# A rounding moved from VectorE to ScalarE in the edge loop of a graph transformer

## What is computed

```python
rel_t = last_update[src] - t
rel_t_enc = jnp.cos(rel_t[:, None] * time_w[None, :] + time_b)      # 32 values for each edge
edge_attr = jnp.concatenate([rel_t_enc, msg], axis=-1)              # 32 + 64
k = k_all[src].reshape(-1, HEADS, CH);  v = v_all[src].reshape(-1, HEADS, CH)
e = (edge_attr @ We).reshape(-1, HEADS, CH)
alpha = jnp.sum(q_all[dst].reshape(-1, HEADS, CH) * (k + e), axis=-1) / math.sqrt(CH)
ex = jnp.exp(alpha - segment_max(alpha, dst)[dst])
out = segment_sum((v + e) * (ex / segment_sum(ex, dst)[dst])[:, :, None], dst)
```

## Time and profile before

| | before |
|---|---|
| three runs, us | 9613.65, 9630.29, 9636.99 |
| median, us | 9630.29 |
| the profiled execution, us | 9621.89 |
| its span, first to last instruction, us | 9620.2 |
| mean granted TensorE clock | 0.825 |
| DVE busy, us (share) | 8650.1 (90%) |
| PE busy | 7559.8 (79%) |
| POOL busy | 6405.7 (67%) |
| ACT busy | 5089.7 (53%) |
| first layer's loop on DVE, from the first `ve_stage` to the last `sum_stage`, us | 378 to 4960 |

### The profile page before, as it was taken

The page is one execution under the profiler, slowest core; times in us unless marked ns, Lnnn a source line. Parts: engine busy times, 40 slices in busy tenths (PEclk is TensorE's granted clock), DMA queues, the critical chain, the costliest instruction groups (busy, mean ns, idle before and its releaser), DMA issues. The chain is left out here.

```text
span 9620.2 us, 272103 instructions
## 1 busy us (share of the span) xinstructions
PE 7559.8 (79%) x52868; PEld 7071.2 (74%) x52869; DVE 8650.1 (90%) x21303; ACT 5089.7 (53%) x20838; POOL 6405.7 (67%) x6871
## 2 busy tenths in 40 slices
PE   6477777887778777787757777888888888888865
PEld 2477777777777777777746777788888888888854
DVE  5899999999999999999987666799999999999968
ACT  2277777777777777777743333333333333333300
POOL 0477777777777777777735777777777777777720
PEclk8699999999999999999975555688888888887888
DMA  6477776777777777777732222455555555555554
GB/s 196 106 185 186 183 181 182 187 183 185 183 182 185 185 184 184 185 184 183 182 85 72 74 74 74 115 151 151 151 153 151 153 150 152 151 153 148 151 139 116
DMA packets 1631706, 1484.67 MB, mean 154 GB/s; under 512 B 792007, under 2 KB 1363043, under 8 KB 1631203
## 3 DMA queue, kind: packets, MB, share of 16 engines
q1 hardware_dynamic: 1374244, 848.34, 35.9%
q0 software_dynamic: 257088, 632.95, 23.6%
HBM read 1225.51 MB, written 254.87 MB: 154 GB/s over the span
## 5 line engine op out<-in xcount | busy, mean ns | idle before, releaser
L818 POOL DMA_INDIRECT kv<-kv_scratch,arena x3136 | 3110.7, 992 | 1272.7 <-issue 832.9
L870 POOL DMA_INDIRECT message_scratch<-ohT,idx x3232 | 3099.2, 959 | 1090.5 <-issue 952.6
L1262 ACT ACTIVATE ohT<-bank,kv 128x128 f32<-128x128 f32 x3232 | 921.1, 368 | 2613.5 <-PE bank L1064 1832.3
L1155 ACT ACTIVATE arena<-arena,weights 128x65 f32<-128x65 f32 x7040 | 1772.1, 337 | 10.7 <-PE bank L983 8.7
L1078 PE MATMUL bank<-oh,kve 128*128 128x128 f32 x8640 | 1377.6, 320 | 141.5 <-DVE arena L1842 108.1
L1064 PE MATMUL bank<-acc,oh 128*128 x6464 | 1287.0, 362 | 208.5 <-ACT ohT L1263 207.9
L1078 PEld LDWEIGHTS bank<-oh,kve 128*128 128x128 f32 x8640 | 1231.1, 224 | 164.9 <-issue 152.0
L1064 PEld LDWEIGHTS bank<-acc,oh 128*128 128x128 f32 x6464 | 1144.1, 266 | 253.5 <-issue 253.1
L983 PE MATMUL bank<-arena,oh 128*128 128x130 f32 x7040 | 1009.4, 288 | 317.1 <-DVE acc L1674 296.7
L983 PEld LDWEIGHTS bank<-arena,oh 128*128 128x128 f32 x7040 | 906.7, 200 | 377.4 <-ACT arena L1155 182.1
L964 PE MATMUL bank<-We,featT 96*128 96x128 f32 x7040 | 1067.3, 299 | 125.6 <-ACT featT L1162 122.1
(11 more groups left out here) (234 smaller groups left out, 12888.7 us busy)
## 6 DMA issues: line engine op xcount, KB each, us to landing
kve<-message_scratch SPq DMA_DIRECT2D x2160, 129.0 KB
kve<-nodes_scratch SPq DMA_DIRECT2D x880, 256.0 KB
feat<-in_edge_attr_dram SPq DMA_DIRECT2D x880, 96.0 KB
feat<-block_scratch SPq DMA_DIRECT2D x812, 98.0 KB
arena<-q_scratch SPq DMA_DIRECT2D x880, 64.0 KB
message_scratch<-ohT,idx POOLq DMA_INDIRECT x3232
kv<-kv_scratch,arena POOLq DMA_INDIRECT x3136
feat<-in_edge_attr_dram SPq DMA_DIRECT2D x880, 32.0 KB
```

The costliest lines, as they stand in the source:

```text
L818: pool.indirect_dma_start(kv[:, k, g, :], None, kv_d, bass.IndirectOffsetOnAxis(ap=group_rows[:, half, k * G + g, 0:1].bitcast(I32), axis= ...
L870: pool.indirect_dma_start(msg_d, bass.IndirectOffsetOnAxis(ap=idx[:, k, g:g + 1], axis=0), sum_ring[:, k % RING1, g, :], None).then_inc(s_ ...
L1155: op = act.activation(wv[:, st.k % 2, g, h, :], vR[:, st.k, g, h, :], ACT.Copy, scale=weights[:, st.k // ROUND, g, st.k % ROUND, h:h + 1])
L1262: act.activation(sum_ring[:, st.k % RING1, g, 0:C], banks[2 + st.k % 2][:, g * P:(g + 1) * P], ACT.Copy, scale=taken[:, st.k, g, 2:3])
```

## The change

The second angle operation, adding MAGIC, leaves DVE. ACT does it, as an Identity activation with a bias tile that holds MAGIC, in a new stage `whole_stage`, which stands behind `featc_stage` and ahead of `weigh_stage` in even iterations. It waits for the first angle operation and counts on a semaphore of its own, `s_whole`. Its result `turns` lies in SBUF (in `arena`), no longer in PSUM. DVE's last angle operation, now `angle(1)`, waits for `s_whole` and comes behind `product_stage`. ANG becomes 2.

```diff
+        magic = sb("magic", [P, 1])
...
+        turns = room(BATCH * G * TD).rearrange("p (b t) -> p b t", t=TD)
...
-        turns = banks[7][:, 2 * P:2 * P + BATCH * G * TD].rearrange("p (b t) -> p b t", t=TD)
...
-        ANG = 3
+        ANG = 2
...
+            def whole_stage(st):
+
+                act.wait_ge(s_ang, ANG * st.batch() + 1)
+                act.activation(turns[:, :, :], encodings(st), ACT.Identity, bias=magic[:, :]).then_inc(s_whole, 1)
...
-                    sines = [(sine_stage, 16)] if k % BATCH == 0 else []
+                    wholes, sines = ([(stage_of, 16)] if k % BATCH == 0 else [] for stage_of in (whole_stage, sine_stage))
...
-                    at(i, k, (arg_stage, 18), *smalls, (featc_stage, 15), (weigh_stage, 2), *sines, *gaps, *exps)
+                    at(i, k, (arg_stage, 18), *smalls, (featc_stage, 15), *wholes, (weigh_stage, 2), *sines, *gaps, *exps)
...
+            dve.memset(magic[:, :], MAGIC)
...
                     if n:
-                        dve.wait_ge(s_ang, done + n)
+                        dve.wait_ge(s_whole, st.batch() + 1)
...
-                    elif n == 1:
-                        wait(dve, s_ang, done)
-                        op = dve.tensor_scalar(t, a, MAGIC, None, ALU.add)
                     else:
                         op = dve.scalar_tensor_tensor(out=a, in0=t, scalar=MAGIC, in1=a, op0=ALU.subtract, op1=ALU.subtract)
...
-                    at(i, k, *turn[0], (ve_stage, 14), *turn[1], (block_stage, 0), (ke_stage, 14), *turn[2], (sum_stage, 0),
-                       (onehotT_stage, 15), *once(5, forward_stage), (product_stage, 13), *once(5, backward_stage), *once(4, run_stage, first_stage),
+                    at(i, k, *turn[0], (ve_stage, 14), (block_stage, 0), (ke_stage, 14), (sum_stage, 0),
+                       (onehotT_stage, 15), *once(5, forward_stage), (product_stage, 13), *turn[1], *once(5, backward_stage), *once(4, run_stage, first_stage),
```

More of the change, by code:

```diff
@@ L348, in build @@
         s_seg = sems("s_seg", MT // SEGMENT)
-        s_rows0 = sems("s_rows0", 2)
+        s_rows0, s_whole = sems("s_rows0", 2), sem("s_whole")
         s_segi, s_acc1 = (sem(n) for n in ("s_segi", "s_acc1"))
```

## The result

The changed kernel takes 9688.16 us (median of four, 9683.98 to 9705.89) against 9624.6 us for the kernel before, run beside it: a ratio of 1.0064, with a 95% interval of 1.0052 to 1.0075. It is **slower by 0.64%, some 60 us**, where 90 us less were forecast.

The account below looks back on a forecast made before the run. DVE was taken to bound the kernel, busy 95% of the first-layer loop. 166 us gained less 62 wait, 10 overlap and 4 waking gave 90 us less: 9540 us as median, range 9464 to 9645 for 8 in 10.

Parts of the forecast that it names:

- L1510's removal: DVE, first-layer loop: taking the rounding off saves 0.377 us in each of 440 batches, 166 us.
- the later sine: ACT's sine comes later, delaying PE's e product for DVE; costed at nothing, 2 us at most in iteration 6.
- Nothing else of DVE hides this: Claim that L1510's removal counts in full, 166 us, since DVE had no idle time around it.
- The move behind the multiplication: DVE's last angle operation, moved behind product_stage, costs what it cost, 0.33 us; nothing added, 4 us either way.
- The addition on ACT: The rounding takes 0.50 us on ACT, 0.43 us of its queue, 189 us in all, absorbed by ACT's idle time.
- the Trainium skill's rule against adds on ScalarE: Adds belong on VectorE; by the rule alone the change loses 35 us, chance 0.02, counted within rival 2.
- The wait for the rounding: DVE's last angle operation waits for ACT in iterations 4, 6, 12, 14: 62 us, plus 10 overlap and 4 waking.
- just used up: Iteration 6, rounds without a wait: the later sine needs 0.76 us against 0.74 spare; costed at nothing.
- Rival 2: PE's longer idle time brings 14 us more low clock each round, 165 us in all: 9705 us, chance 0.10.
- the three rivals: Wait takes it all, 9630 us (0.15); slower by PE's clock, 9705 (0.10); waits are hidden, 9464 (0.10).

Follow-up runs that it names:

- e13_early: e4_block with DVE's last angle operation moved back right behind ke_stage, ahead of block_stage's register load; 9885.61 us, ratio 1.0267 to the kernel before.
- e7_actonly: The kernel before plus one unused 128x256 Identity activation on ACT in each even iteration, at the rounding's place; 9651.98 us, ratio 1.0017.
- e1_head24: The changed kernel with the head of DVE's first-layer loop 24 slots further on, its closing branch 28 places behind a multiple of 256; 9579.02 us, ratio 0.9954.
- e4_block: e1_head24 with block_stage, a register load on DVE's sequencer, moved behind ke_stage; 9572.52 us, ratio 0.995 to the kernel before.
- e18_beforewarm: The kernel before with PE's e matmuls in iterations 1, 2, 9, 10 and aggregation matmuls in 4, 6, 12, 14 done twice; 9568.9 us, ratio 0.9948.
- e14_warm: e4_block with PE's e matmuls in iterations 1, 2, 9, 10 and aggregation matmuls in 4, 6, 12, 14 done twice; 9508.73 us, ratio 0.9875.
- e15_both: e4_block with the rounding first in ACT's even iterations, and the sine ahead of the weighings in iterations 6 and 14; 9511.78 us, ratio 0.9872.
- e17_all: e15_both with the doubled PE matmuls of e14_warm added; 9576.99 us, ratio 0.9957 to the kernel before.

## Why the prediction was wrong, step by step

The step that failed first is one that the prediction put at nothing without a word: that DVE's loop, 24 instructions shorter, otherwise runs as before. Its closing branch cost 96 us more. Behind it two terms of the sum were wrong: L1510's removal gave 41 us less than its 166, and the later sine, put at nothing, cost 28. The details:

- **L1510's removal, 166 us: right as a reading, 41 us too much as a gain.** 2.99 us a pass, 164 us, is what its start-to-start distances gave. "Nothing else of DVE hides this" was true, and the reverse had been left out: **L1510 hid something itself.** The prediction looked for idle time around L1510 and found none, because L1510 covered the register load of `block_stage` where the sequencer had no lead. That the 0.48 and 0.41 us in iterations 0, 2 and 10 were longer than the usual 0.33 was used for a larger gain, and it was the sign of the load beneath: 41 us. The rows of iteration 0 even have 0.06 us of idle time behind L1510 (2515.66 + 0.42 = 2516.08 against 2516.14).
- **The move behind the multiplication costs nothing: right**, L1516 takes 416 ns, and L1512 took 414. e13_early shows that it is worth some 300 us as against waiting behind `ke_stage`.
- **The addition on ACT, 0.50 us each: right; no effect of its own: nearly right.** The row after:

```profile
L1168 ACT ACTIVATE arena<-feat,magic 128x256 f32<-128x256 f32 x440 | 218.5, 497 | 7.4 <-DVE feat L1514 5.0 <-issue 1.1
```

  e7_actonly puts the added work alone at +0.17%, 16 us, at most 30. The prediction had drawn 35 us from the Trainium skill's rule against adds on ScalarE ("ScalarE: Activation LUTs", "Rules for kernel authors"); e7_actonly stays below this.
- **The wait for the rounding, 62 + 10 + 4 = 76 us: the size right** (0.97 x 55 = 53 us in the changed kernel, 62 in e1_head24), the places half right: iterations 6 and 14, as said, but nothing in 4 and 12, where 17 us had been put; only 0.15 us a pass of another kind was lost there. One in iteration 6 (DVE, then ACT):

```profile
2537.91 0.68 DVE L1545 TENSOR_TENSOR y_all<-kve,bank 128x512 f32<-128x512 f32 x1
2539.39 0.42 DVE L1516 SCALAR_TENSOR_TENSOR feat<-arena,feat 128x256 f32<-128x256 f32 x1 [0.80 <-ACT arena L1168]
```

```profile
2538.38 0.57 ACT L1163 ACTIVATE featT<-bank 96x512 f32<-96x512 f32 x1
2538.86 0.49 ACT L1168 ACTIVATE arena<-feat,magic 128x256 f32<-128x256 f32 x1
```

  The copy, then the rounding ending at 2539.35, then DVE at 2539.39 behind 0.80 us of idle time: the mechanism and the very size that had been worked out from the round at 2420 us.
- **The later sine, costed at nothing: wrong.** 0.74 us had been found spare in iteration 6, "just used up", and more than 1.5 us in all others. The wait for `e` came in iteration 8: 0.69 us of it in the changed kernel, 1.08 in e1_head24. The sine of iteration 6 ends 8.04 us behind its batch's first angle operation instead of 7.42, and that of iteration 8 5.67 instead of 3.59. The prediction had counted ACT's delay once for each batch (0.43 us); it had not followed it through DVE's wait into the next batch, nor through PE's clock: behind 1.81 us of idle time PE's `e` took 1.54 us here, and 1.55 to 1.64 us on average in the products that `ve_stage` takes up in iterations 0, 6 and 8, where 1.11 had been assumed:

```profile
2539.01 1.54 PE L965 MATMUL bank<-We,featT 96*128 96x128 f32 x8 [1.81 <-ACT featT L1163]
...
2543.15 1.09 PE L957 MATMUL bank<-ident,feat 128*96 128x128 f32 x4 [0.87 <-ACT feat L1174]
```

  Net +0.51 us a pass, 28 us, some 0.14 of it ahead of acc. In e7_actonly, where nothing but ACT's delay was added, the waits for `e` grew too, in iterations 0, 6, 8 and 14.
- **Rival 2, PE's clock:** its mechanism is there and not at its size. The clock fell from 0.91 to 0.89 in the stretch of the earlier trace rows, and what the doubled products take away of it in e4_block is worth 0.75%, 72 us; but over two thirds of that (0.52% by e18_beforewarm) was there before. It would not have made the kernel slower.
- **What made it slower isn't in the prediction at all:** the loop's closing branch, 1.88 us x 51 = 96 us. The prediction costed the removed instructions by what lies around them in time, and nowhere by what their number does to the program. The pause was in the trace of before, 0.46 us behind each closing branch, and so was the count of instructions in the body, 541.

The sum as it should have been: 164 - 53 (rounding) - 41 (register load) - 28 (`e`) - 8 (one-hot) = 34 us less, and with the branch 96 us more: 62 us slower. None of the three rivals names this. That rival 2's 9705 us lies near the measured 9688 is chance: its mechanism, PE's clock, isn't what took the time. With the branch where it had been, the changed kernel is 0.46% faster than before (e1_head24); with the register load covered and PE busy, or with ACT's order mended instead, 1.25% and 1.28% (e14_warm, e15_both). These two are the fastest kernels of this study, ahead of before and after.

**What stays open.** Why the pause is 0.46 us and no less where the branch stands far behind a multiple of 256, whether it is a fetch and when that starts, and why the pause differs between 2.35 and 1.83 us at the same place. Why PE's low clock stands in other iterations after the change. What e17_all lost it to.

## What to carry to other kernels

Before taking an instruction out of an engine that bounds, ask what it covers: a register load or a wait of the sequencer beneath it costs nothing only as long as something is queued ahead, and it shows in a start-to-start distance longer than that of its sisters. Where a hardware loop's body has hundreds of instructions (here 541 and 517), count them before and after each edit: a pause that appears ahead of the first instruction of the body may belong to the branch, whatever releaser the profile names, and moving the loop's head is a test that touches no work. Where two waits of like size stand one behind the other, taking one away shows the other; judge such edits in pairs, and check the pair by a run, since edits that gain alone can lose together.

## What was not expected of the hardware

- A taken branch at the end of a body of 517 or 541 instructions was followed by a pause of 2.35 or 1.83 us with the branch 4 places behind a multiple of 256, 1.37 us at 12 and 0.46 us at 28 and at 104. A change of 24 instructions in a body that runs 52 times moved the kernel by 1.1%.
- The profile names for such a pause the semaphore that was raised last, here ACT's L1185 with 108 us; in e1_head24 the same line has 3.6.
- 14% more matmuls on PE, all of them idle work, made the kernel before 0.52% and e4_block 0.75% faster, together with a higher granted clock (0.92 to 0.96 and 0.89 to 0.94 in the stretch 400 to 4850 us).
- A wait of DVE for ACT moved forward by a few instructions, from behind the product to behind `ke_stage`, cost 230 us instead of 80, and 80 us more ahead of acc, where a register load stood behind the wait.
